# A two-layer block with six interleaved streams: the delta rule's early part moved by one period, and its triangular inverses built from 64x64 tiles

## The reference, cut to what matters

```
k = k * rsqrt(sum(k * k) + 1e-12);  beta = sigmoid(x @ Wb)
for t in range(n):
    delta = (v_t - k_t^T S) * beta_t
    S = S + k_t delta^T
    o_t = q_t^T S
```

## Time and profile before

| | us |
|---|---|
| median of 3 runs | 2267.91 (2267.54 to 2269.87) |
| the profiled execution | 2270.01 |
| its span, first to last instruction | 2268.0 |
| TensorE busy | 1957.7 (86%) |
| VectorE busy | 1401.9 (62%) |
| ScalarE busy | 947.8 (42%) |
| GpSimd busy | 824.7 (36%) |

### The profile page before, as it was taken

How to read it: one execution, slowest core, us unless ns; L and a number is a source line. 1 busy time by engine, 2 the same in 40 slices (tenths; PEclk the granted TensorE clock), 3 DMA queues, 4 the chain that set the end, 5 groups by cost and what they waited for, 6 DMA issues and landing times. The chain is left out here.

```text
span 2268.0 us, 40783 instructions
## 1 busy us (share of the span) xinstructions
PE 1957.7 (86%) x15104; PEld 1291.3 (57%) x15104; DVE 1401.9 (62%) x3394; ACT 947.8 (42%) x2465; POOL 824.7 (36%) x823
## 2 busy tenths in 40 slices
PE   3797779998899988998899988998799988998686
PEld 1594448564685557654585557654585556754332
DVE  3553465775758756775757756775767847674442
ACT  1413442365424652265424643265514653264023
POOL 4506550444406541443506542353505442160000
PEclk9788898999899998999899998999999998999557
DMA  4200012100311012200302012100212012100200
GB/s 167 50 20 15 17 35 62 53 14 15 77 36 41 18 40 61 53 14 15 78 24 54 18 38 64 53 14 11 71 31 57 14 31 74 47 16 1 75 1 6
DMA packets 124820, 89.71 MB, mean 40 GB/s; under 512 B 42168, under 2 KB 111928, under 8 KB 124344
## 3 DMA queue, kind: packets, MB, share of 16 engines
q1 hardware_dynamic: 124016, 85.39, 14.0%
q0 software_dynamic: 320, 1.05, 0.1%
q10 hardware_dynamic: 288, 0.67, 0.1%
HBM read 46.84 MB, written 25.17 MB: 32 GB/s over the span
## 5 line engine op out<-in xcount | busy, mean ns | idle before, releaser
L1636 POOL TENSOR_TENSOR soft<-soft,prec 128x512 f32<-128x512 f32 x128 | 135.7, 1066 | 541.6 <-DVE prec L1295 540.5
L1163 ACT ACTIVATE shared<-bank 128x512 f32<-128x512 f32 (+1 forms) x384 | 202.7, 528 | 254.3 <-PE bank L931 252.3
L1447 DVE TENSOR_REDUCE nmx<-bank 128x1 f32<-128x512 f32 (+3 forms) x352 | 224.6, 638 | 105.3 <-PE bank L909 104.4
L1083 ACT ACTIVATE soft<-bank,nmax 128x128 f32<-128x128 f32 x512 | 180.2, 384 | 169.4 <-DVE nmax L1287 168.7
L1597 POOL TENSOR_TENSOR qk_rs<-qk_rs,minus_half 128x16 f32<-128x16 f32 x64 | 187.8, 2935 | 5.3
L930 PE MATMUL bank<-b_sb 128*128 128x128 bf16 x512 | 118.0, 231 | 41.6 <-ACT shared L1163 39.7
L931 PE MATMUL bank<-shared 75*128 75x384 bf16 (+3 forms) x512 | 149.5, 318 | 0.0
L621 PE MATMUL bank<-w_sb,hT 128*128 128x512 f32 x256 | 136.7, 620 | 8.7 <-DVE hT L1237 5.7
L909 PE MATMUL bank<-shared 72*128 72x256 bf16 (+3 forms) x512 | 135.9, 317 | 0.0
L1595 POOL TENSOR_SCALAR rs_f<-mv_f 128x4 f32<-128x4 f32 x24 | 5.6, 234 | 344.2 <-DVE mv_f L1226 344.2
L593 PE MATMUL bank<-c_sb,soft 128*128 128x128 f32 x608 | 106.3, 308 | 27.5 <-POOL soft L1636 22.4
(11 more groups left out here) (236 smaller groups left out, 4809.1 us busy)
## 6 DMA issues: line engine op xcount, KB each, us to landing
shared<-parts_dram SPq DMA_DIRECT2D x64, 288.0 KB
vm<-v_f SPq DMA_DIRECT2D x112, 128.0 KB, 2.3
parts_dram<-parts SPq DMA_DIRECT2D x96, 128.0 KB, 2.5
L_dram<-shared SPq DMA_DIRECT2D x32, 256.0 KB, 2.5
shared<-X_dram SPq DMA_DIRECT2D x32, 256.0 KB, 3.0
shared<-L_dram SPq DMA_DIRECT2D x32, 256.0 KB, 3.8
w_sb<-weights SPq DMA_DIRECT2D x1, 4167.0 KB, 21.2
x_tm<-x SPq DMA_DIRECT2D x8, 256.0 KB, 3.1
```

The source lines that it names most:

```text
L1083: a = af(v4(p_sb, 2, 4)[:, j, g], place("fS", j)[:, g * P:(g + 1) * P], ACT.Exp, bias=nmax[:, at:at + 1], accum_out=psums[:, at:at + 1])
L1163: af(v4(PTm, 2, GROUP)[:, u % 2, i, 0:n], place("mST")[:, 0:n], ACT.Exp).then_inc(mexp_done, 1)
L1447: reduce(v3(nmx[:], HM)[:, h:h + len(heads), c], v3(place("mS")[:, 0:len(heads) * (c + 1) * P], len(heads)), AX, ALU.max, negate=True).the ...
L1636: tt(p, p, spread(prec[:, at:at + NPAIR], P), ALU.mult).then_inc(fnorm_done, 1)
```

## The change

A seventh stream, e, takes the delta rule's steps from the head norm through `k`, `krs`, `beta`, `kT`, `gram`, `solve` to the store of the inverted blocks, for sequence p + 1 in period p (and for sequence 0 in period -1, where each engine does its f steps and then its e steps). kT, kn and blk move out of the overlaid memory, L is built in the experts' buffer `the`. `bg` splits into `beta` (early) and the gate. Keys, beta, kT and gram share PSUM bank 3, which the experts use. All strings of `ORDER` are new. In them TensorE begins a period with the four `qT`, `bg`, `mq` and the first `fS`, then takes the inverses among steps of all other streams, and puts the key steps among the scores and values of the second half; VectorE has `solve` between `fw2` and `x1` of layer 1; SP has the loads of X and L behind `final` and the load of x, and the first `send` behind the load of chunk 2; experts 0 to 3 stand ahead of the first score step `mS`, where experts 0 and 1 without its last product stood. The inverses at levels 1 and 2 become products of two 64x64 tiles on the diagonal (r = 0, 1), with the 32 of 64 columns that are new at this level, and VectorE adds or masks those alone; at level 3 one 64x64 tile per head makes the new block, and it is copied instead of added. In the setup SP zeroes `X_dram` instead of GpSimd. Left out below: semaphores' names, walk tables, and edits that only follow from others.

```diff
-STREAMS = "fbdacm"
+STREAMS = "fbdacme"
 ORDER = {
     "PE": (
-        "ddbddfdfddmmddfddmdddbbddbfbffbdddfmfdbbmbfmbfffbmmbdbmbdddbdddddddddbdddmdmdddbdbdddbdddddddddddbdddbdmdddbdb"
-        "dbbbbbdmabamfafamdfamfafamfamafaffabafmfaamacbcfacmacbacacbacmacbacfacacbcafcfamacbcbaccbacfcabcafcacfacbcafcf"
-        "amabccacfcabcmcabcacbcabcafcfamabccabcmcabcfabccafcbcfcmcccfcbccfbccbbbbbfcbccbccccccbccc"),
+        "dddddmbdfmfddmdbfdbdbdbdffmdfdbdmddddmdfdbbdmddbmdbddffdmdfdbfddedmbdbdbdbddmfmbdmdddmdbbmdbmdbmdbddmmdbmabbma"
+        "bbababbdamfaafmfafafamamafffbamfacfacmacbbabcacacfbfacfamacbaecffabccbaecbefcbacceaccffcaecaffabcfafaccaecbaeb"
+        "cabcbaccfcbacefeafcacbbcaceacbcafcaccabcafcebfaceccacecbaccbbbcbcbccbcbccccbcccccccccbc"),
...
     "DVE": (
-        "ddbdddbmddbfdmfmmddmbmddbfbmbfmdddbmbmbbmmmmddbdddddddddbdddbmbmdddddddddddddddddbbdddbmdbdddbbbbmadbamafamfam"
-        "afamafamaafabamabfabmaamaaamabaaabababmafacafabaaafbabafabmafamacababababmafafamabbabfbcmfbbbbbbbcc"),
+        "debmdmbfddbmddmdfmmdddbdmbddbdmddbdmmfdfddbddmmdemddmbdbdbddmddbdmdmbddmdbdbmmmbdbdddbmbmmbmdaaabbabembamafafa"
+        "mafamafmababamabafmaafaabamababbaaffeefaaebaeacababaabafafbeabaababfaafcaeaabbaebaebaebabcbbbebcbc"),
...
     "SP": (
-        "mddfdddfddmddaffafaffafafc"),
+        "edddmdffmaafffafaeeeeafeefc"),
...
+def steps_early(b):
+
+    s = (steps_head(b) if b else []) + [("k", b, c) for c in range(NT)] + [("krs", b), ("beta", b)] + [("kT", b, c) for c in range(NT)]
+    return s + [("gram", b, c) for c in range(NT)] + [("solve", b), ("keep", b)]
+
+
 def steps_delta(b):
 
-    s = [("k", b, c) for c in range(NT)] + [("krs", b)] + [("bg", b, c) for c in range(NT)]
-    s += [("kT", b, c) for c in range(NT)] + [("gram", b, c) for c in range(NT)]
-    s += [("qT", b, h) for h in range(H0)] + [("solve", b)]
+    s = [("qT", b, h) for h in range(H0)] + [("bg", b)]
...
-        return {s: steps_head(0) + steps_chunks(0, 0, 0, AHEAD) if s == "f" else [] for s in STREAMS}
+        first = {"f": steps_head(0) + [("hcopy", 0)] + steps_chunks(0, 0, 0, AHEAD), "e": steps_early(0)}
+        return {s: first.get(s, []) for s in STREAMS}
...
-                "m": steps_moe(p - 1) if late else []}
+                "m": steps_moe(p - 1) if late else [], "e": steps_early(p + 1) if p + 1 < BATCH else []}
...
-        for s in ORDER[engine]:
+        for s in ORDER[engine] if p >= 0 else [s for s in STREAMS for _ in left[s]]:
...
-        delta = [("kT", NT * T), ("qT", NT * T), ("Z", NT * T), ("L", 2 * T), ("X", 2 * T),
-                 ("kn", NT * T), ("gs", T), ("Vm", 2 * T), ("Bm", T), ("blk", 3 * BLK * BLK), ("th", NT * NBG), ("o_all", T)]
+        kT, kn, blk = sb("kT", NT * T), sb("kn", NT * T), sb("blk", 3 * BLK * BLK)
+        Lx = the
+
+
+        delta = [("qT", NT * T), ("Z", NT * T), ("X", 2 * T), ("L", 2 * T), ("Bm", T), ("gap", 3 * T), ("Vm", 2 * T), ("o_all", T), ("gs", T), ("th", T)]
...
-            "k": lambda c: c % 2, "bg": lambda c: c % 2, "kT": lambda c: c % 2, "G": lambda c: c % 2,
-            "qT": lambda h: h % 2, "V": lambda k, c: c % 2, "VX": lambda k, c: c % 2, "ZV": lambda k, c: 2,
+            "k": lambda c: 3, "beta": lambda: 3, "kT": lambda c: 3, "G": lambda c: 3, "bg": lambda: 0,
+            "qT": lambda h: h % 2, "V": lambda k, c, r=0: ((0, 0), (0, 1), (0, 1), (1, 1))[k][r] if c % 2 == 0 else ((2, 2), (2, 0), (2, 0), (2, 2))[k][r],
...
+                sp.wait_ge(zeroed, 2)
+                for c in range(NT):
+                    sp.dma_start(in_dram(X_dram, c), v3(zeros, H0)).then_inc(X_zeroed, 16)
+                sp.wait_ge(X_zeroed, 16 * NT)
...
+        def tile(ap, r):
+
+            return ap[64 * r:64 * r + 64, :, 64 * r:64 * r + 64]
+
+        def half(ap, k, upper):
+
+            return ap.rearrange("p h (m two b) -> p h m two b", two=2, b=BLK << (k - 1))[:, :, :, int(upper)]
+
+        def product(name, k, c, r):
+
+            at = ("V", "ZV", "VX").index(name) * P
+            return place("V", k, c, r)[64 * r:64 * r + 64, at:at + P].rearrange("p (h m b) -> p h m b", h=H0, b=BLK << (k - 1))
+
+        def last_product(name, c):
+            at = ("V", "ZV").index(name) * 2 * P
+            return v3(place("V", LEVELS - 1, c)[0:64, at:at + 2 * P], H0)
...
                         if b > 1:
-                            pe.wait_ge(mPV_psum, GROUPS * 3 * (b - 1))
-                    if c >= 2:
-                        pe.wait_ge(ksq_done, NT * b + c - 1)
+                            pe.wait_ge(eh_done, (NE + 1) * (b - 1))
+                    else:
+                        pe.wait_ge(ksq_done, NT * b + c)
...
+                def beta_(b):
+                    pe.wait_ge(ksq_done, NT * (b + 1))
+                    for c in range(NT):
+                        m = mm(place("beta")[:, c * H0:(c + 1) * H0], xnT[:, c * P:(c + 1) * P], W("wbg")[:, 0:H0], start=True, stop=True)
...
-                    pe.wait_ge(kT_copied, NT * b + min(c + 3, NT))
-                    if c >= 2:
-                        pe.wait_ge(L_done, NT * b + c - 1)
+                    if c:
+                        pe.wait_ge(L_done, NT * b + c)
+                    else:
+                        pe.wait_ge(kT_copied, NT * (b + 1))
...
+                    if h == 0:
+                        pe.wait_ge(head_copied, b + 1)
+                        if b:
+                            pe.wait_ge(oT0_copied, b)
+                        if b > 1:
+                            pe.wait_ge(mPV_psum, GROUPS * 3 * (b - 1))
+                    if h >= 2:
                         pe.wait_ge(qT_copied, H0 * b + h - 1)
+                def bg(b):
+                    pe.wait_ge(qT_copied, H0 * b + 3)
+                    for c in range(NT):
+                        m = mm(place("bg")[:, c * P:(c + 1) * P], xnT[:, c * P:(c + 1) * P], W("wbg")[:, H0:NBG], start=True, stop=True)
+                    m.then_inc(bg_psum, 1)
...
-                            m = mm(ps[:, h * P:(h + 1) * P], Lc[:, h], Zc[:, h], start=True, stop=True)
+                            if k == LEVELS - 1:
+                                m = mm(last_product("V", c)[:, h], Lc[64:P, h, 0:64], Zc[64:P, h, 64:P], start=True, stop=True)
+                                continue
+                            for r in range(2):
+                                m = mm(product("V", k, c, r)[:, h], tile(Lc, r)[:, h], half(tile(Zc, r), k, True)[:, h],
+                                       start=True, stop=True, skip_group_check=True)
...
-                        m = mm(ps[:, h * P:(h + 1) * P], Xc[:, h], Vc[:, h], start=True, stop=True)
+                        if k == LEVELS - 1:
+                            m = mm(last_product("ZV", c)[:, h], Xc[0:64, h, 0:64], Vc[0:64, h, 64:P], start=True, stop=True)
+                            continue
+                        for r in range(2):
+                            m = mm(product("ZV", k, c, r)[:, h], tile(Xc, r)[:, h], half(tile(Vc, r), k, True)[:, h],
+                                   start=True, stop=True, skip_group_check=True)
...
-                            m = mm(ps[:, h * P:(h + 1) * P], Vc[:, h], Xc[:, h], start=True, stop=True)
+                            for r in range(2):
+                                m = mm(product("VX", k, c, r)[:, h], tile(Vc, r)[:, h], half(tile(Xc, r), k, False)[:, h],
+                                       start=True, stop=True, skip_group_check=True)
...
                         pe.wait_ge(xn2_copied, b + 1)
+                        pe.wait_ge(L_done, NT * min(b + 2, BATCH))
...
+                    nc.vector.tensor_copy(xnT[:], place("hT")[:]).then_inc(head_copied, 1)
+
+                def hcopy(b):
+                    dve.wait_ge(head_copied, b + 1)
+                    if b:
                         dve.wait_ge(fv_psum, ch(b, 0, 0))
-                    nc.vector.tensor_copy(xnT[:], place("hT")[:])
-                    nc.vector.tensor_copy(hT[0:64, :], place("hT")[0:64, :])
-                    nc.vector.tensor_copy(hT[64:P, 1:T], place("hT")[64:P, 0:T - 1]).then_inc(head_copied, 1)
+                    shifted(hT, xnT).then_inc(hT_copied, 1)
...
+                    Vc = v4(Vm, 2, H0)[:, c % 2]
+                    if k == LEVELS - 1:
+                        ts(Vc[0:64, :, 64:P], last_product("V", c), -1.0, None, ALU.mult).then_inc(Vm_done, 1)
+                        return
+                    nc.vector.memset(half(Vc, k, False), 0.0)
                     mask = repeat(B("lowT")[:, (k - 1) * P:k * P], H0)
-                    tt(v4(Vm, 2, H0)[:, c % 2], v3(place("V", k, c)[:], H0), mask, ALU.mult).then_inc(Vm_done, 1)
+                    for r in range(2):
+                        m = tt(half(tile(Vc, r), k, True), product("V", k, c, r), half(tile(mask, r), k, True), ALU.mult)
+                    m.then_inc(Vm_done, 1)
...
-                    dve.wait_ge(ZV_psum, NT * (LEVELS - 1) * b + at_level(k, c, LEVELS - 1, 1) + 1)
+                    if k == LEVELS - 1:
```

(27 more changed lines are left out.)

133 lines of the change are left out of this document (65 added, 68 removed).

## The result

The changed kernel takes 2211.2 us in the median of four runs (2193.57, 2209.86, 2212.5, 2229.32), the kernel before on the same chip 2268.9 (2267.54 to 2270.38). The ratio is 0.972, with a 95% interval of 0.966 to 0.978: 2.8% faster (2.5% by the medians), inside the range that was given, but 62 us above the forecast of 2149. All ratios and intervals of this document leave out the runs more than 1.5% above the fastest of the same kernel (2229.32 here), while the medians take all runs in. The runs of the kernel before lie within 3 us of each other, those of the changed kernel within 36; that spread is the first hint at what is missing. The profiled execution of the changed kernel is the fastest of the four: 2193.57 us, with a span of 2191.8.

The account below looks back on a forecast made before the run. It took a full period as bound by TensorE's work plus some 24 us idle, both ends by chains. Periods -134, period 7 -8, start +10, tail +13 sum to -119: 2151 us profiled, 2149 median, range 2075 to 2250.

Parts of the forecast that it names:

- The full period: Periods 1 to 7: -19.2 us each from 257.4, hence 238 us, with TensorE 93% busy.
- The early part: Delta rule's steps moved one period up, among scores and values: 7 us idle and 3 of clock back, +1 for the solve.
- -7 for the hole: First quarter of a full period: 7 of TensorE's 10.9 us idle time come back, ends 0 and 14.
- -3 for the clock: First quarter of a full period, clock 0.87: fewer holes raise it; 3 of 8 us lost work come back.
- +1 for the solve: VectorE's solve between `fw2` and `x1` delays x1 by 10.8 us; scores and values cover TensorE, +1 us stays.
- the 10 of the forecast: Sign of being right: the inverses come within 10 us of a period's start.
- The tiles: Inverses of a full period: 32 tiled groups at 0.47 us take 15.0 us instead of 30.1, saving 15.1.
- 4 for the switches: Switching between tiles and full array: about 20 runs a period at 0.2 us, 4 us; ends 0 and 10.
- The start: First early part in line before period 0: first X load near 97, then 205 us; +10 us, ends -10 and +30.
- The tail: Last stretch: four experts ahead delay the first score product 25 us; half stays, +13 us, ends 0 and +25.
- slower by the clock: Rival, chance 0.07: half-width tiles lower the inverse stage's clock, costing 65 f a period; 2307 us at f = 0.3.
- the signs of being wrong: Tiled groups near 0.9 us; 5 us holes at x1 or X loads; inverse-stage clock under 0.8; period 0 over 230 us.

Follow-up runs that it names:

- early_only: The changed kernel with inverses over the whole array, as in the kernel before; 2243.2 us, ratio 0.990 to the kernel before.
- old_tail: The changed kernel, but its last period alone walks the order strings of the kernel before; 2178.3 us, ratio 0.956 to the kernel before.
- tiles_only: The kernel before with the tiled inverses of the changed one, its own streams, order and memory; 2307.7 us, ratio 1.019.
- b_twice: old_tail with each product of `seq_b` (keys' and queries' B, in the inverse stage) issued twice; 2169.9 us, ratio 0.958 to the kernel before.
- level3_whole: old_tail with both products of level 3 over the whole array again, levels 1 and 2 still tiled; 2159.3 us, ratio 0.954 to the kernel before.
- level3_twice: old_tail with each tiled product of level 3 issued twice; 2168.1 us, ratio 0.958 to the kernel before.
- gram_twice: old_tail with each `gram` product of the early part, late in the period, issued twice; 2231.8 us, ratio 0.976 to the kernel before.
- tiles_twice: The changed kernel with each tiled product of levels 1 and 2 issued twice; 2306.6 us, ratio 1.016 to the kernel before.
- old_tail_again: The same kernel as old_tail, measured again on another chip; 2169.3 us, ratio 0.955 to the kernel before.

## Why the prediction was right and where it was not

**The full period: 238 forecast and 239.0 measured** where the clock holds. The sum agrees better than its terms do, and that is luck in part: TensorE's busy time fell by 233.6 - 215.7 = 17.9 us, where 13.2 was forecast (15.1 - 4 - 0.9 + 3), and the idle time, forecast to fall by 6, is where it was. TensorE is 90% busy in the period, not 93%. By steps:

- The early part: -7 for the hole, -3 for the clock, +1 for the solve, and +0.9 for the split of `bg`, which early_only has too: -8.1 in all; early_only measured -8.4. The place of the gain was right too. The first load of X (second row below) is issued 2 us into the period, and the first inverse product of level 1 stands at 572.6, 11.4 us into the period (the 10 of the forecast, nearly); before, the load came 53 us into it.

```profile
562.60 0.51 SPq L1762 DMA_DIRECT2D x_tm<-x  x1
563.22 0.49 SPq L1796 DMA_DIRECT2D shared<-X_dram  x1
```

- The idle time of a period did not shrink, though: 239.0 - 215.7 = 23.3 us, as before (256.9 - 233.6 = 23.3). Cut at the end of the inverses (630.5), it lies elsewhere:

```profile
569.20:630.50 61.30, 57.61 (x826) 44.96 (x824) 46.90 (x143) 26.07 (x83) 25.13 (x26) 1.00 0.18 51
630.50:777.00 146.50, 132.57 (x1102) 81.54 (x1103) 104.41 (x245) 79.73 (x205) 74.26 (x72) 1.00 0.14 34
777.00:800.20 23.20, 17.53 (x105) 11.65 (x104) 12.79 (x52) 6.64 (x14) 2.29 (x3) 0.78 0.10 18
```

  3.7 us in the first 69 us, where the first quarter had 10.9 in 64: the -7 of the forecast, to the us. But 13.9 in the long middle and 5.7 in the last 23 us, which has a granted clock of 0.78. That the chains of scores now stand with less TensorE work beside them would explain it, but no run isolates it. Two groups of the score and value products, TensorE in period 2 of the changed kernel, hold 8.1 us of the 23.3; both wait for ScalarE's exponents:

```profile
L979 PE MATMUL bank<-b_sb 128*128 128x128 bf16 x64 | 14.3, 223 | 4.4 <-ACT shared L1219 4.3
...
L994 PE MATMUL bank<-shared,vaug 128*32 128x512 f32 (+3 forms) x128 | 11.1, 441 | 3.7 <-ACT shared L1219 3.7
```

  Of the 8.4 us of the early part, 5.7 are busy time of TensorE (233.6 to 227.9 in early_only) and some 2 idle time, which the tiles gave back. The clock of the first quarter (0.87 before, 1.00 in the pieces above) accounts for a part of the 5.7; the rest I do not place. The sum was right, the split between idle time and busy time was not.
- The tiles: -15.1 + 4 for the switches, -11.1 in all; 249.0 to 239.0 is -10.0, of which 1 to 3 are the better clock. The group of levels 1 and 2 was priced 0.47 and took 0.49 to 0.56 with its share of switches. Level 3 was priced at 0.47 and took 0.48 where another group follows; its eight groups with the ways out come to 4.75 us in place of 3.8. The ways out of the tiles that the lines above show come to 0.07, 0.11 and 0.35 us (0.56, 1.07 and 1.31 less their groups), where 0.2 was priced. TensorE's busy time fell by 12.2 us against early_only, so that switches and longer groups together cost 15.1 - 12.2 = 2.9 us in place of 4; the idle time, which rose by 2, was in no term. A record of the groups of levels 1 and 2 takes 0.49 / 16 = 0.031 us. The Trainium skill (TensorE: Matmul & The Clock Gate, "Wait - 56ns, not 53.3ns?") gives some 62 ns for each matmul where the sequencer decodes in firmware; these records are shorter, so that it does not bind them, as the prediction had it. The Trainium skill (TensorEngine Tiling (Array Packing), Key Properties) says that a change of the tiling mode drains TensorE; by the numbers above the changes cost something here, but less than the 4 us of the sum.
- **The start**: +10 forecast, +10.9 measured. The first X load came at 106.3 us, where 97 was in the sum, and period 0 ended 197 us after it, where 205 was: two misses, of 9 and of 8 us, that cancel.
- **The tail**: +13 forecast, +16.3 measured, and old_tail shows that the order of the last period is the cause, with the first score product back at its old place. That product stands at 2065.6, 63.9 us into its stretch, where it was 41.8 before: 22 us later, 25 forecast. Rather more than half of it was left over: 16 of 22.

**The step that failed is the clock of the inverse stage.** The sum took -3 us for a better clock, and nothing for a worse one; the rival "slower by the clock" named the very mechanism (half-width tiles with 32 columns bring the lower level in full periods) and its place, and got 0.07. One of the signs of being wrong, a clock under 0.8 in the inverse stage, did appear in two periods (0.63 and 0.50 in the pieces of period 5). The rival's price was 65 f a period, for a share f of 65 us of work. A fall costs 13.2 us, so f is 0.20 in the period that has one; the two of the profiled execution cost 32 us, and over the rival's eight periods f is 32 / (8 x 65) = 0.06, far below the 0.23 from which it decides. So the outcome lies between the forecast and that rival, nearer to the forecast. Two falls explain 13.2 + 19.1 = 32 of the 43 us between -119 and -76 in the profiled execution (the 19.1 of period 1 with its other stretches at the lower clock); the tail gives 3, the periods 1 us each 5, period 7 (231.8 for 230) 2, the start 1. The median run lies 18 us above the profiled one at a lower mean clock, which would be one fall more or a little over (argued). Without its two falls the profiled execution would have taken some 2193.6 - 32.3 = 2161 us, an estimate, against a forecast of 2151 for it. The 2149.3 of old_tail is no proof of the forecast: its last stretch is 23 us shorter, and a run of 2151.2 of the same kernel still has a fall.

The evidence against the rival was read wrongly. I held the score tiles at clock 0.99 against it; they fill four tiles at once, the inverses' products one at a time or two by turns with 32 columns. The row that spoke for it was period 0 at 0.66 with TensorE 95% busy: the kernel before, too, has stretches in which TensorE is nearly always busy and the clock is low. It is no row of small tiles, though. Its products are mostly over the whole array, many of them those of `seq_b` to `seq_o` (L844 to L881) with 32 or 128 columns. The timeline of the kernel before in that row, where groups of eight go from 1.06 to 2 us:

```profile
128.56 1.06 PE L844 MATMUL bank<-shared 128*128 128x128 f32 x8
...
134.14 2.05 PE L844 MATMUL bank<-shared 128*128 128x128 f32 x8
...
142.47 1.92 PE L881 MATMUL bank<-U_sb,shared 128*128 128x32 f32 x8
```

In the changed kernel the falls, too, begin where these steps follow level 3. So the row does not tell how much the tiles matter.

**Not settled**: what the chip weighs when it lowers the clock. Shown is that the tiled inverses bring the falls (tiles_only against before, the changed kernel against early_only), that with twice the tiled work at levels 1 and 2 each of the six full periods of the profile has one (one of the six runs, 2285.8 us against 2306.6, will have had fewer), and that 2 to 4 us more work in the stage, whole (b_twice, level3_whole) or tiled (level3_twice), goes with no fall of 30.7 us, while the same work elsewhere (gram_twice) does not. tiles_twice and level3_twice both add tiled work to the stage and end on opposite sides, and in b_twice the clock drops at the usual place and comes back after 3.4 us; no run here says why. Periods 2 and 5 of the changed kernel run alike for 30 us and part all the same, so something beside the instructions of the period takes part. Not tried was a delay without work in the place of the added products, nor whether products of the whole array woven between the tiled groups, at equal work, would hold the clock.

## What to carry to other kernels

Price small tiles by the clock as well as by the record. Look in the profile of before for a stretch that is over 90% busy and yet at the lower clock, as the earlier trace rows has it: there a busy engine is no argument that the clock will hold, and the price of a fall belongs in the sum. No run here gives a measure by which a fall can be foretold; how much of the array the products fill is a suspicion. If the runs of a kernel spread by more than those of the kernel before do, look at the granted clock of like periods side by side before any theory on waits, and look also for short drops at the place of the long ones. When a sum comes out right, compare its terms too: here idle time and busy time missed in opposite ways. Where a kernel ends with a period that has lost half of its streams, give that period an order of its own: one more set of strings was worth 23 us here.

## What the hardware showed that was not expected

- TensorE's granted clock can fall for 30.7 us with the engine 99% busy, after the same 30 us of instructions that keep it in another period; a period with one was 13 to 19 us longer. In the same kernel on the same chip, times went from 2149.3 to 2196.1 us, with the mean clock from 0.932 to 0.907.
- More work need not cost time: b_twice adds 32 needless records a period to old_tail (3.4 us more in a period without a fall), and its median, 2169.9, equals old_tail_again's 2169.3 on another chip, with a worst run of 2175.7 in place of 2196.1.
- A change that nearly halves TensorE's work in a stage can make a kernel slower: tiles_only, 1.019 [1.017, 1.020].
- Two tiles by turns, 32 columns each, take 0.031 us a record; a single tile with 64 columns takes 0.48 / 8 = 0.060.
